# Reordering the ramp of a two-layer pipeline: early grams, products between delta chunks, a packed block stored in halves, weight pieces spread out

## The chip, the cores and the metric

The kernel runs on one core of one Trainium2 chip. The metric is the device time of one launch in microseconds. Three runs of the kernel before gave 913.12, 915.89 and 917.56 us: median 915.89.

## The reference, cut to what matters

Input is x of shape (4, 1024, 128): 4 sequences, 1024 tokens, 128 channels. Two layers follow, each an attention-like block and a feed-forward block, each with a residual and a layer norm behind it.

```python
# layer 0, attention: a delta rule with 4 heads of 32, in chunks of 32 tokens
q, k, v = (silu(causal_depthwise_conv(x @ W.T, taps)) for W, taps in ...)   # 4 taps
beta = sigmoid(x @ Wb.T); q, k = l2norm(q), l2norm(k); v, k_beta = v * beta, k * beta
attn = -(k_beta @ k.T) * strictly_lower                 # per chunk, 32 x 32: the "gram"
for i in range(1, 32): attn[i] += attn[i] @ attn        # the "solve", row by row
u, w = (attn + I) @ v, (attn + I) @ k_beta
for each chunk: u_new = u_i - w_i @ S; o_i = q_i @ S + attn_i @ u_new; S = S + k_i.T @ u_new
# o is mixed with v by a gate, normed by head, and goes through Wo
# layer 0, feed-forward: 8 experts (128 -> 256 -> 128, gelu), the best two weighted by a router
# layer 1, attention: a gated linear scan over time; a = exp(-8 softplus(a_param) sigmoid(..))
# layer 1, feed-forward: a gated unit 128 -> 512, two hidden 512 x 512 layers, 512 -> 128
```

## The kernel before, in words

The tokens are cut into NT = 8 tiles of 128 tokens of all 4 sequences, 512 columns each; channels lie on the partitions. Every fp32 product is made of three matmuls on parts (high times low, low times high, high times high; mm3), so activations and weights are split into a high and a low half by DVE, ACT and POOL.

**Stages.** Five engines each run their own written-out order of instructions (PE, ACT, DVE, POOL, and SP for the DMAs); they meet only in semaphores. The **lead** (for t in range(LEAD), LEAD = 5, in each engine's block) prepares tiles 0 to 4: project (q, k, v products with 12 matmuls each, banks 0 to 2), beta (bank 3), squares (banks 4 and 5), the norms on ACT (norms_ln, norms_exp), unit_rows (q and k scaled, transposed) and value_rows, key_spread (the keys copied per head on ACT, L826), gram (16 matmuls of 128x64 in two halves g = 0, 1, banks 6 and 7, L460), and gram_rows (DVE reads the grams out). The result is a packed block pks[t] that store_pack (L322) writes to memory in one DMA of 1280 KB.

Two tiles together go through a **solve** on POOL (L1090): 31 steps of a multiply and a subtract, each step needing the one before. solve_in (L1269) turns the grams for it, solve_out (L1276) turns its result back and scales it. Solve 0 is for tiles 0 and 1, solve 1 for 2 and 3, solve 2 for 4 and 5, solve 3 for 6 and 7. From its result t_spread (POOL, texp) makes the stationary operands of the delta rule.

**schedule** (L265) then runs, on every engine: ramp1(a=0, s=5), ramp2(a=0, s=6), dense(0, a=1), ramp3(m=0, a=1, s=7), dense(1, ...), tails and so on. a is the tile whose delta rule or attention end is computed, s the tile that is prepared, m the tile in the experts, f the tile in the last feed-forward. ramp1 runs the four chunks of tile 0's delta rule (delta_wu, delta_attn, delta_state on PE; delta_spread, delta_qp, delta_out on DVE; then mix, mix_end) around the preparation of tile 5. ramp2 does the head norm, attention_out, the layer norm, router, top_two, gate_weights and gate_rows of tile 0 around tile 6. dense(m, a, f) loops over the 8 experts: up, gate_rows, one step of tile a's delta rule, down of the expert before; ACT makes two gelus of each half, one in high precision (hf) and one rounded (fbh); DVE subtracts for fbl slot 0, POOL for slot 1. ramp3 is like ramp2, with tile 7 and the scan of layer 1.

**Weights** come in 19 pieces of 512 columns through two buffers (ws); load_piece (SP, L315) waits until DVE has split the piece before in the same buffer (split_pieces, L1297). Pieces 0 to 3 and 8 are centred or scaled as well (five DVE instructions instead of two). PIECES (L33) says which tile's step splits which pieces. load_xs brings a tile of x, split_x splits it.

**Shared memory.** pk2, the packed block of tiles 4 to 7 (12288 bytes a partition), lies over fbh (8192 bytes at at_fb) and the first two slots of fbl behind it; so the first rounded gelu of dense(0) waits for the store of tile 6's block (L977), and that of dense(1) for tile 7's. PE enters dense(0) only when gram_read of tile 6 is complete (L661). softplus_log (L1324) is a chain of 24 DVE instructions on one column; its result, spv, is first used by lru_decay (ACT, L891) in ramp3.

Of the kernel before, what the change touches and what calls it, by code (L numbers as in the profile page):

```python
# [14 lines left out]
NH, DK, C = 4, 32, 32  # L15
# [17 lines left out]
PIECES = ((0, 1), (2, 3), (4, 5), (6, 7, 8), (9, 10, 11), (12,), (13, 14, 15), (16, 17, 18))  # L33
PIECE_BUF = tuple(p % 2 for p in range(NPIECE))
LEAD = 5

# [10 lines left out]
def build(nc, io):  # L47
    ctx = ExitStack()
    with ctx:
# [73 lines left out]
        fbh = sb("fbh", [128, FC, W], F32R); fbl = sb("fbl", [128, FC, W], F32R)  # L123
# [59 lines left out]
        def low_of(p):  # L183
# [3 lines left out]
        names = """w_in cst_in conv_in x_in pk_stored pk_loaded tb_in fw_in ws_in0 ws_in1 ws_hi ws_lo xs_in tt_stored  # L187
            ws_sum ws_mean ws_cen s3_row s3_read cen_ready w3_scaled wo_sum wo_mean wo_cen
            wtap_f wtap_hi wtap_done xt_hi xt_ready
            beta_proj qkv_proj qkv_act sq_done ss_done rs_ln rs_act kq_done kt_done vt_done kexp_done gram_done  # L190
# [60 lines left out]
        def x_slot(t):  # L251
            return 1 if t % 2 == 0 and t < LEAD else 0

# [35 lines left out]
        def _(sp):  # L289
# [32 lines left out]
            def store_pack(t):  # L322
                need(sp, "gram_read", 2 * t + 2)
                need(sp, "kt_done", t + 1)
                need(sp, "vt_done", t + 1)
                need(sp, "pk_stored", 16 * (t - 1))
                sp.dma_start(io["pack"][:, t * CT:(t + 1) * CT, :, :], pks[t][:, :, 1:, :]).then_inc(S["pk_stored"], 16)
# [19 lines left out]
            for t in range(LEAD - 1):  # L347
                load_xs(t + 2)
                for p in PIECES[t][2:] + PIECES[t + 1][:2]:
                    load_piece(p)  # L350
                if t:
                    store_pack(t)
            for p in PIECES[LEAD - 1][2:]:
                load_piece(p)
# [9 lines left out]
            def ramp1(a, s):  # L364
                load_xs(s + 1)
                for p in PIECES[s]:
                    load_piece(p)
                store_pack(s)

            def ramp2(a, s):  # L370
                for p in PIECES[s][:2]:
                    load_piece(p)
                load_xs(s + 1)
                load_next(a + 1)
                store_tt(1)
                for p in PIECES[s][2:] + PIECES[s + 1][:2]:
                    load_piece(p)
# [6 lines left out]
            def dense(m, a, f, inv=0):  # L384
                if isinstance(m, int) and m == 0:
                    load_piece(PIECES[NT - 1][2])
# [19 lines left out]
        def _(pe):  # L406
# [13 lines left out]
            def beta(t):  # L420

                pe.wait_ge(S["xs_in"], 16 * t + 16)
                if t < LEAD:
                    need(pe, "bt_ready", t)
                    bk = 3
                else:
# [3 lines left out]
                    bk = 7  # L430
                mm(by_seq(bank[bk][:, :]), wsm[:, 0, :], xs[:, :, HALO:HALO + TOK]).then_inc(S["beta_proj"], 1)

            def project(t, m):

                pe.wait_ge(S["xt_ready"], t + 1)
                if t < LEAD:
# [5 lines left out]
                else:  # L442
# [3 lines left out]
                o = m if t < LEAD else 4 + m  # L446
# [6 lines left out]
            def squares(t):  # L453

                for m in range(2):
                    pe.wait_ge(S["sq_done"], 2 * t + m + 1)
                    need(pe, "rs_ln", 2 * (t - 1) + m + 1)
# [1288 lines left out]
```

## Time and profile before

| | us |
|---|---|
| median of 3 runs | 915.89 |
| profiled execution | 913.16 |
| its span, first to last instruction | 911.2 |
| PE busy | 815.4 (89%) |
| DVE busy | 618.1 (68%) |
| ACT busy | 490.4 (54%) |
| POOL busy | 481.7 (53%) |
[...]

The stages lie as follows: lead to 99.8 us, ramp1 from there to about 141, ramp2 to about 173, dense(0) to about 229, ramp3 to about 275, then dense(1) and the rest. Busy shares are averages over all stages. [...]

### The profile page before, as it was taken

Reading aid. Unit: us, or ns where it says so; the run is one execution under the profiler, and the core shown is the slowest. Engines: PE = TensorE matmul, PEld = TensorE weight load, DVE = VectorE, ACT = ScalarE, POOL = GpSimd, SP = SyncE. Lnnn points to the kernel's source line nnn. Section 1 sums busy time; section 2 is a strip of 40 time slices with the busy share of each in tenths; the row PEclk is TensorE's granted clock in tenths of the full one; section 3 lists DMA queues with packets and bytes.
Section 4 is the critical chain, followed back from the end, with each engine's and each line's share of the span. In section 5 each row is a group of like instructions: output and inputs, shape, how many; then the busy total and the mean of one; then the engine's idle time right before and its main releaser. Section 6 shows DMA issues by size and latency. Waiting matters only on the chain.

```text
span 911.2 us, 11908 instructions
## 1 busy us (share of the span) xinstructions
PE 815.4 (89%) x3810; PEld 627.9 (69%) x3810; DVE 618.1 (68%) x1166; ACT 490.4 (54%) x768; POOL 481.7 (53%) x508
## 2 busy tenths in 40 slices
PE   5998797688858999899989999999999999999996
PEld 3776584576547767776777678767876886766664
DVE  2777975677357768776876687767767767677352
ACT  3877147042744466357535653574466447667553
POOL 0059696577523744983586345435644454266333
PEclk9998799589959999999999999999999999999999
DMA  3143606300302030003000400120020000000000
GB/s 127 47 115 96 184 2 178 111 12 1 82 0 82 1 82 1 1 0 93 1 1 2 116 0 2 27 66 0 0 69 23 0 0 12 1 0 13 1 12 12
DMA packets 37727, 35.81 MB, mean 39 GB/s; under 512 B 1584, under 2 KB 30512, under 8 KB 37680
## 3 DMA queue, kind: packets, MB, share of 16 engines
q1 hardware_dynamic: 37680, 35.22, 13.8%
q8 instruction: 25, 0.41, 0.2%
q14 instruction: 22, 0.18, 0.1%
HBM read 21.85 MB, written 13.37 MB: 39 GB/s over the span
## 4 chain that ended last, share of the span: by engine, by line
PE 56%; DVE 15%; issue 10%; POOL 10%; ACT 6%; DMA 2%; POOLq 0%; DVEq 0%; ACTq 0%; SPq 0%
PE bank L408 56%; POOL tpm L1105 2%; POOL tmp L1102 2%; POOL fbl L1161 2%; POOL acc L1169 2%; DVE sexp L1401 2%; DVE spread L1385 1%; DVE yg L1411 1%; DVE m L1446 1%; POOL fbl L1192 1%; ACT L1056 1%; DMA pack<-pk 1%; POOL fal L1200 1%; DVE fah L1631 1%; DMA ws<-in_wf 1%
## 5 line engine op out<-in xcount | busy, mean ns | idle before, releaser
L975 ACT ACTIVATE hf<-bank 128x512 f32<-128x512 f32 x64 | 38.3, 598 | 178.5 <-PE bank L408 171.1
L1161 POOL TENSOR_TENSOR fbl<-hf,fbh 128x512 fp32r<-128x512 f32 x64 | 81.9, 1280 | 91.1 <-DVE fbh L1574 91.1
L1102 POOL TENSOR_TENSOR tmp<-apm,tpm 128x31 f32<-128x31 f32 (+15 forms) x124 | 77.5, 625 | 52.8 <-DVE apm L1274 45.6
L1192 POOL TENSOR_TENSOR fbl<-hf,fbh 128x512 fp32r<-128x512 f32 x32 | 41.3, 1290 | 103.2 <-DVE fbh L1631 103.2
L408 PEld LDWEIGHTS bank<-pk,spread 128*128 128x128 f32 x640 | 82.3, 206 | 19.6 <-DVE spread L1385 13.8
L408 PE MATMUL bank<-pk,spread 128*128 128x64 f32 x640 | 85.0, 290 | 8.2 <-DVE spread L1385 7.3
L1572 DVE TENSOR_TENSOR fbl<-hf,fbh 128x512 fp32r<-128x512 f32 x64 | 59.5, 930 | 39.3 <-ACT fbh L979 39.2
L1105 POOL TENSOR_TENSOR tpm<-tpm,tmp 128x31 f32<-128x31 f32 (+15 forms) x124 | 77.9, 628 | 9.7
L1169 POOL TENSOR_TENSOR acc<-acc,yg 128x512 f32<-128x512 f32 x48 | 64.4, 1341 | 32.4 <-DVE yg L1411 32.4
L408 PE MATMUL bank<-fal,wfh 128*128 128x512 f32 x160 | 68.3, 427 | 2.7 <-ACT hf L1005 1.6
L1188 POOL TENSOR_TENSOR fal<-hf,fah 128x512 fp32r<-128x512 f32 x32 | 41.7, 1302 | 51.7 <-DVE fah L1626 51.7
L1411 DVE TENSOR_TENSOR yg<-bank,gb 128x512 f32<-128x512 f32 x64 | 43.9, 685 | 34.5 <-PE bank L408 34.4
L408 PE MATMUL bank<-fbl,wmh 128*128 128x512 f32 x128 | 58.7, 459 | 8.3 <-POOL fbl L1161 4.9
L1005 ACT ACTIVATE hf<-bank,vec 128x512 f32<-128x512 f32 x64 | 42.5, 686 | 42.4 <-PE bank L408 42.1
L1200 POOL TENSOR_TENSOR fal<-hf,fah 128x512 fp32r<-128x512 f32 x32 | 41.4, 1299 | 40.6 <-DVE fah L1631 40.6
L408 PE MATMUL bank<-fah,wfh 128*128 128x512 f32 x160 | 62.6, 391 | 0.0
L408 PE MATMUL bank<-fah,wfl 128*128 128x512 f32 x160 | 62.4, 390 | 0.0
L408 PE MATMUL bank<-fbl,wfh 128*128 128x512 f32 x128 | 55.2, 431 | 7.5 <-POOL fbl L1192 7.5
L408 PE MATMUL bank<-x1l,wmh 128*128 128x512 f32 x128 | 55.5, 433 | 2.8 <-ACT fbh L979 1.6
L408 PE MATMUL bank<-x1h,wmh 128*128 128x512 f32 x128 | 52.0, 406 | 0.0
L408 PE MATMUL bank<-x1h,wml 128*128 128x512 f32 x128 | 51.7, 404 | 0.0
L408 PE MATMUL bank<-fbh,wfh 128*128 128x512 f32 x128 | 51.4, 401 | 0.0
(219 smaller groups left out, 2232.7 us busy)
## 6 DMA issues: line engine op xcount, KB each, us to landing
pack<-pk SPq DMA_DIRECT2D x7, 1280.0 KB, 6.8
pk<-pack SPq DMA_DIRECT2D x7, 1280.0 KB, 7.2
ws<-in_wf SPq DMA_DIRECT2D x11, 256.0 KB, 2.9
xs<-in_xh SPq DMA_DIRECT2D x8, 262.0 KB, 3.6
xt<-in_xh SPq DMA_DIRECT2D x8, 262.0 KB, 3.0
ws<-in_wm SPq DMA_DIRECT2D x8, 256.0 KB, 2.7
tt<-ttp SPq DMA_DIRECT2D x4, 512.0 KB, 2.8
out<-f SPq DMA_DIRECT2D x8, 256.0 KB, 2.5
```

The source lines that it names most:

```text
L408: return P.matmul(out, lhsT, rhs, start=start, stop=stop, skip_group_check=skip)
L975: A.activation(hf[:, 0, :], bank[4][:, :], ACT.Gelu).then_inc(S["gelu_done"], 1)
L1005: A.activation(hf[:, o % 2, :], bank[4 + o][:, :], ACT.Gelu, scale=vec[:, v + o:v + o + 1])\
L1102: G.tensor_tensor(m, a, r, ALU.mult).then_inc(S["t_mul"], 1)
L1105: G.tensor_tensor(o, o, m, ALU.subtract).then_inc(S["t_step"], 1)
L1161: G.tensor_tensor(fbl[:, s, :], hf[:, 1, :], f32(fbh[:, s, :]), ALU.subtract)\
L1169: G.tensor_tensor(acc[:, :], (x1 if e == 1 else acc)[:, :], yg[:, (e - 1) % 2, :], ALU.add)\
L1188: G.tensor_tensor(fal[:, c, :], hf[:, c % 2, :], f32(fah[:, c, :]), ALU.subtract)\
L1192: G.tensor_tensor(fbl[:, o, :], hf[:, o % 2, :], f32(fbh[:, o, :]), ALU.subtract)\
L1200: G.tensor_tensor(fal[:, o, :], hf[:, o % 2, :], f32(fah[:, o, :]), ALU.subtract)\
L1411: tt(yg[:, e % 2, :], bank[6][:, :], gb[:, e % 2, :], ALU.mult).then_inc(S["yg_ready"], 1)
L1572: tt(fbl[:, s, :], hf[:, 0, :], f32(fbh[:, s, :]), ALU.subtract).then_inc(S["lo0"], 1)
```

## The change

It reorders the lead and the ramps and moves three kinds of buffers. The list, by engine:

- **Lead, PE:** tile 0's and tile 1's squares, products and grams stand in a new order; the four grams run right behind project(2, 0). In the last round PE also does beta(5), project(5, 0) and project(5, 1). squares(1) uses banks 6 and 7. Tile 5's beta and products use banks 3, 0, 1 and 3; tile 6's beta is in bank 1, its third product in bank 0.
- **Lead, POOL:** it makes the second half of the keys' copies of tiles 0 and 1 (kexp_pool), two instructions of 128x1024.
- **Lead, DVE:** solve_in(0) comes right behind tile 1's grams; solve_out(0) stands in the last round ahead of piece 8 and tile 4's gram_rows; softplus_log leaves for ramp3; split_x(6) comes at the end.
- **ramp1, ramp2:** below in the diff. From ramp2's DVE order solve_out(1), one piece and split_x(7) go to dense(0), solve_in(2) and two pieces go ahead of head_scale. solve_init(2) and the first ten solve steps leave POOL's ramp2 for dense(0).
- **dense(0):** solve_out(1) at e = 1, split_x(7) at e = 3, pieces at e = 2, 4, 5, 6; two solve steps per expert at e = 1 to 6.
- **Packed block:** fbl and fbh change places in memory, and the rounded halves use slots in the other order (high_slot), so that expert 0's do not lie under the block. Blocks 5 < t are stored in two halves (pk_half, pk_stored).

```diff
-PIECES = ((0, 1), (2, 3), (4, 5), (6, 7, 8), (9, 10, 11), (12,), (13, 14, 15), (16, 17, 18))
+PIECES = ((0, 1), (2, 3), (4, 5), (6, 7), (8,), (9, 10), (11, 12, 13), (14, 15, 16), (17, 18))
-        fbh = sb("fbh", [128, FC, W], F32R); fbl = sb("fbl", [128, FC, W], F32R)
+        fbl = sb("fbl", [128, FC, W], F32R); fbh = sb("fbh", [128, FC, W], F32R)
+        def low_slot(e):
+            return (e % 2) * HC
+        def high_slot(e):
+            return ((e + 1) % 2) * HC
...
             def store_pack(t):
+                if t > LEAD:
+                    need(sp, "gram_read", 2 * t + 1)
+                    need(sp, "pk_half", 16 * (t - LEAD - 1))
+                    c0 = 8
+                    sp.dma_start(io["pack"][:, t * CT:t * CT + c0, :, :], pks[t][:, 0:c0, 1:, :])\
+                        .then_inc(S["pk_half"], 16)
                 need(sp, "gram_read", 2 * t + 2)
...
# PE, lead
-            for t in range(LEAD):
+            squares(0)
+            beta(1)
+            project(1, 0)
+            project(1, 1)
+            squares(1)
+            project(1, 2)
+            beta(2)
+            project(2, 0)
+            gram(0, 0)
+            gram(0, 1)
+            gram(1, 0)
+            gram(1, 1)
+            project(2, 1)
+            project(2, 2)
+            for t in range(2, LEAD):
                 squares(t)
...
+                else:
+                    beta(t + 1)
+                    project(t + 1, 0)
+                    project(t + 1, 1)
                 gram(t, 0)
                 gram(t, 1)
# PE, ramp1 (whole, after)
+                project(s, 2)
+                pe.wait_ge(S["qkv_act"], 3 * LEAD + 2)
                 delta_wu(a, 0)
+                squares(s)
                 delta_attn(a, 0)
                 delta_state(a, 0)
                 delta_wu(a, 1)
+                project(s + 1, 0)
                 delta_attn(a, 1)
                 delta_state(a, 1)
                 delta_wu(a, 2)
+                gram(s, 0)
                 delta_attn(a, 2)
                 delta_state(a, 2)
                 delta_wu(a, 3)
+                gram(s, 1)
                 delta_attn(a, 3)
                 delta_state(a, 3)
+                pe.wait_ge(S["qkv_act"], 3 * LEAD + 3)
+                mix_gate(a)
+                beta(s + 1)
                 project(s + 1, 1)
# PE, ramp2: project(s, 2) ahead of attention_out; dense(0) waits for gram_read behind up(m, 0)
# ACT, lead: tiles 0 and 1 together
+            for m in range(3):
+                heads_in(0, m)
+            beta_in(0)
+            heads_in(1, 0)
+            heads_in(1, 1)
+            beta_in(1)
+            A.preload_act_table_set(LN_EXP)
+            norms_ln(0)
+            norms_ln(1)
+            norms_exp(0)
+            norms_exp(1)
...
+            key_spread(0, 0)
+            key_spread(1, 0)
+            heads_in(1, 2)
# ACT, lru_decay, tile 0
+                    act.wait_ge(S["ws_lo"], NPIECE)
+                    act.wait_ge(S["sp_step"], SP_STEPS)
# DVE, lead
+            beta_rows(0)
+            value_rows(0)
+            split_x(2)
+            split_pieces(PIECES[0][:1])
+            beta_rows(1)
+            unit_rows(0)
+            unit_rows(1)
+            split_pieces(PIECES[0][1:2])
+            gram_rows(0, 0)
+            gram_rows(0, 1)
+            gram_rows(1, 0)
+            gram_rows(1, 1)
+            solve_in(0)
...
+                if t == LEAD - 1:
+                    solve_out(0)
+                split_pieces(PIECES[t])
                 gram_rows(t, 0)
                 gram_rows(t, 1)
-            solve_out(0)
-            softplus_log()
+            split_x(LEAD + 1)
# DVE, ramp1
                 delta_spread(a, 0)
-                split_pieces(PIECES[s])
+                beta_rows(s)
...
                 delta_spread(a, 1)
+                split_pieces(PIECES[s][:1])
+                unit_rows(s)
                 delta_qp(a, 1)
-                split_x(s + 1)
...
                 delta_spread(a, 3)
+                split_pieces(PIECES[s][1:])
...
                 mix_end(a)
+                value_rows(s)
                 gram_rows(s, 1)
# DVE, ramp2 (whole, after)
+                solve_in(2)
+                split_pieces(PIECES[s][:2])
                 head_scale(a)
                 unit_rows(s)
+                beta_rows(s)
                 attention_norm(a)
                 top_two(a)
+                value_rows(s)
+                gram_rows(s, 0)
                 gate_weights(a)
+                gram_rows(s, 1)
                 gate_rows(a)
# DVE, ramp3: behind scale("2")
+                split_pieces(PIECES[NT])
+                softplus_log()
# DVE, dense(0)
+                    if isinstance(m, int) and m == 0 and e == 1:
+                        solve_out(1)
+                    if isinstance(m, int) and m == 0 and e == 3:
+                        split_x(NT - 1)
+                    if isinstance(m, int) and m == 0 and e in (2, 4, 5, 6):
+                        p = (2, 4, 5, 6).index(e)
+                        split_pieces((PIECES[NT - 2][2:] + PIECES[NT - 1])[p:p + 1])
...
+                        if e == 0 and isinstance(m, int) and m in (0, 1):
+                            dve.wait_ge(S["pk_half"], 16 * (m + 1))
# POOL, dense(0) and ramp3
+                    if isinstance(m, int) and m == 0 and e == 1:
+                        solve_init(2)
+                    if isinstance(m, int) and m == 0 and 0 < e < E - 1:
+                        solve(2, range(2 * e - 2, 2 * e))
-                solve(2, range(17, C - 1))
+                solve(2, range(12, C - 1))
```

The SP queue follows the new order: load_xs(6) moves into the lead, the pieces are loaded one tile's step ahead of their splits, store_tt(1) and the last four loads of pieces stand in dense(0).

## Rows read from the trace of the kernel before

**Rows 1.** Stretches: us, busy us of PE, PEld, DVE, ACT, POOL, PEclk, DMA share, GB/s

```profile
22.60:53.00 30.40, 30.35 (x151) 23.52 (x152) 23.59 (x50) 25.17 (x44) 0.00 (x0) 1.00 0.19 53
...
99.80:110.10 10.30, 5.07 (x18) 4.34 (x18) 9.42 (x28) 0.00 (x0) 5.65 (x11) 0.67 0.79 230
...
155.20:167.40 12.20, 8.22 (x40) 8.06 (x40) 10.45 (x13) 2.06 (x3) 9.34 (x16) 0.59 0.30 91
...
176.00:184.00 8.00, 6.63 (x23) 5.80 (x23) 1.07 (x1) 1.15 (x3) 0.00 (x0) 0.50 0.62 166
184.00:229.00 45.00, 39.31 (x203) 32.27 (x203) 37.49 (x65) 16.60 (x33) 34.61 (x31) 0.91 0.03 7
```

**Rows 2.** PE's waits, 79 to 330 us: total, times, longest

```profile
PE bank L408 <- DVE gate L1494: 6.1, 1, 6.1
PE bank L408 <- POOL texp L1131: 5.2, 1, 5.2
```

**Rows 3.** POOL timeline, first and last step of solve 0, then texp

```profile
55.05 0.24 POOL L1102 TENSOR_TENSOR tmp<-apm,tpm 128x31 f32<-128x31 f32 x1 [45.56 <-DVE apm L1274]
...
98.21 0.25 POOL L1105 TENSOR_TENSOR tpm<-tpm,tmp 128x31 f32<-128x31 f32 x1
103.79 2.46 POOL L1131 TENSOR_TENSOR texp<-ttp,cst 128x512 f32<-128x512 f32 x2 [5.33 <-DVE ttp L1285]
```

**Rows 4.** DVE timeline, solve 0's input, piece 8, solve 0's output, first spread

```profile
53.00 1.97 DVE L1274 STREAM_TRANSPOSE apm<-kkp 128x1024 f32<-128x1024 f32 x1
...
86.87 1.10 DVE L1304 TENSOR_TENSOR ws<-ws,s3row 128x512 f32<-128x512 f32 x1
...
90.47 0.96 DVE L1312 TENSOR_TENSOR wfl<-ws,wfh 128x512 fp32r<-128x512 f32 x1
...
100.49 1.90 DVE L1283 STREAM_TRANSPOSE ttp<-tpm 128x1024 f32<-128x1024 f32 x1
...
110.12 1.22 DVE L1385 TENSOR_TENSOR spread<-bank,cst 128x1024 f32<-128x1024 f32 x1
```

**Rows 5.** PE timeline, the lead: start, us, engine line op, idle before and releaser

```profile
24.93 0.80 PE L408 MATMUL bank<-xtl,wtaph 128*128 128x512 f32 x1
...
33.58 0.40 PE L408 MATMUL bank<-xth,wtaph 128*128 128x512 f32 x1
33.81 1.89 PE L408 MATMUL bank<-pk,gb 128*128 128x64 f32 x16
```

**Rows 6.** PE timeline, tile 4 and the start of dense(0)

```profile
81.31 1.94 PE L408 MATMUL bank<-hf,cst 128*128 128x512 f32 x4
87.13 3.65 PE L408 MATMUL bank<-pk,gb 128*128 128x64 f32 x16 [3.88 <-DVE pk L1236]
...
184.19 0.76 PE L408 MATMUL bank<-x1l,wmh 128*128 128x512 f32 x1 [1.41 <-ACT fbh L979]
```

**Rows 7.** DVE timeline, end of ramp1 and x1 in ramp2

```profile
138.03 1.01 DVE L1423 SCALAR_TENSOR_TENSOR a<-a,pk 128x512 f32<-128x512 f32 x1
...
153.37 0.69 DVE L1379 TENSOR_TENSOR x<-bank,a 128x512 f32<-128x512 f32 x1 [3.58 <-ACT a L860]
```

**Rows 8.** DVE timeline, router read, gate done, and lru_input in ramp3

```profile
167.37 0.18 DVE L1463 COPY lg<-bank 128x32 f32<-128x32 f32 x1
...
170.98 0.19 DVE L1494 TENSOR_TENSOR gate<-gt 128x32 f32<-128x32 f32 x1
...
241.85 0.90 DVE L1434 SCALAR_TENSOR_TENSOR m<-m,x 128x512 f32<-128x512 f32 x1 [6.33 <-ACT m L887]
```

**Rows 9.** ACT timeline, the first high half of dense(0)

```profile
183.45 0.60 ACT L979 ACTIVATE fbh<-bank 128x512 fp32r<-128x512 f32 x1 [5.05 <-DMA pack<-pk]
```

**Rows 10.** DVE by line and shape, 184 to 229 us: busy, mean ns, idle

```profile
L1411 DVE TENSOR_TENSOR yg<-bank,gb 128x512 f32<-128x512 f32 x8 | 5.5, 685 | 2.2 <-PE bank L408 2.1
...
L1312 DVE TENSOR_TENSOR wfl<-ws,wfh 128x512 fp32r<-128x512 f32 x3 | 4.3, 1421 | 0.1
```

**Rows 11.** POOL timeline, after ramp3

```profile
280.62 1.28 POOL L1161 TENSOR_TENSOR fbl<-hf,fbh 128x512 fp32r<-128x512 f32 x1 [22.31 <-DVE fbh L1574]
```

More of the change, by code:

```diff
@@ L348, in _ @@
                 load_xs(t + 2)
-                for p in PIECES[t][2:] + PIECES[t + 1][:2]:
+                for p in PIECES[t + 1]:
                     load_piece(p)
@@ L352, in _ @@
                     store_pack(t)
-            for p in PIECES[LEAD - 1][2:]:
-                load_piece(p)
+            load_piece(PIECES[LEAD][0])
+            load_xs(LEAD + 1)
             store_pack(LEAD - 1)
@@ L364, in ramp1 @@
             def ramp1(a, s):
-                load_xs(s + 1)
-                for p in PIECES[s]:
+                load_piece(PIECES[s][1])
+                for p in PIECES[s + 1][:2]:
                     load_piece(p)
@@ L385, in dense @@
                 if isinstance(m, int) and m == 0:
-                    load_piece(PIECES[NT - 1][2])
+                    store_tt(1)
+                    for p in PIECES[NT - 1][1:] + PIECES[NT]:
+                        load_piece(p)
                 if inv == 1:
@@ L605, in ramp1 @@
                 delta_wu(a, 2)
-                squares(s)
+                gram(s, 0)
                 delta_attn(a, 2)
@@ L809, in beta_in @@
                     act.wait_ge(*after("d2", 1))
-                A.activation(btanh[slot(t)], bank[3 if t < LEAD else 7][:, :], ACT.Tanh, scale=0.5).then_inc(S["bt_ready"], 1)
+                A.activation(btanh[slot(t)], bank[beta_bank(t)][:, :], ACT.Tanh, scale=0.5).then_inc(S["bt_ready"], 1)
             def norms_ln(t):
@@ L836, in _ @@
             act.wait_ge(S["w_in"], 32)
-            for t in range(LEAD):
+            for m in range(3):
[9 more added lines that the diff above has]
+            norms_exp(1)
+            act.wait_ge(S["sp_step"], 1)
+            A.activation(spv[:, 1:2], spv[:, 0:1], ACT.Exp, scale=-1.0).then_inc(S["sp_step"], 1)
+            key_spread(0, 0)
+            key_spread(1, 0)
+            heads_in(1, 2)
+            for t in range(2, LEAD):
                 for m in range(3):
@@ L908, in ramp1 @@
             def ramp1(a, s):
-                for c in range(3):
-                    heads_in(s, c)
                 beta_in(s)
+                heads_in(s, 0)
+                heads_in(s, 1)
                 A.preload_act_table_set(LN_EXP)
@@ L1119, in _ @@
             solve_init(0)
+            for t in range(2):
+                pool.wait_ge(S["kq_done"], 2 * t + 2)
+                G.tensor_tensor(kspread[slot(t)][1], rep(pks[t][:, 8:16, SK:SK + 1, :], 2, NH), heads(8), ALU.mult)\
+                    .then_inc(S["kexp_pool"], 1)
             solve(0, range(C - 1))
@@ L1144, in ramp2 @@
             def ramp2(a, s):
-                solve_init(2)
                 t_spread(a + 1, 0)
                 t_spread(a + 1, 1)
-                solve(2, range(10))
             def ramp3(m, a, s):
@@ L1174, in dense @@
                         solve_init(3)
-                    if isinstance(m, int) and m == 0 and e < E - 1:
-                        solve(2, range(10 + e, 11 + e))
+                    if isinstance(m, int) and m == 0 and e == 1:
+                        solve_init(2)
+                    if isinstance(m, int) and m == 0 and 0 < e < E - 1:
+                        solve(2, range(2 * e - 2, 2 * e))
                     if inv == 1 and e >= 3:
@@ L1353, in _ @@
             centre_rows(wsm[:, 2:3, :], wsum[:, 20:21], "wo", 1)
-            for t in range(LEAD):
+            beta_rows(0)
[11 more added lines that the diff above has]
+            solve_in(0)
+            value_rows(1)
+            split_x(3)
+            split_pieces(PIECES[1][:2])
+            for t in range(2, LEAD):
                 unit_rows(t)
                 if t == LEAD - 1:
-                    split_pieces(PIECES[t - 1][2:])
                     solve_in(1)
```

129 lines of the change are left out of this document (61 added, 68 removed).

## The prediction

> **What bounds the kernel now.** I read three views in this order. The table by stretches shows that the lead is TensorE's own: 30.35 of 30.40 us busy at full clock [rows 1]. The ramp after it is not: between 99.8 and 110.1 PE works 5.07 of 10.3 us, between 155.2 and 167.4 it waits much of the time while DVE is busy for 10.45 of 12.2 us, and from 176 to 184 everything except PE stands nearly still and PE runs at half clock (PEclk 0.50) [rows 1]. PE's waits name what it waited for longest: the gate from DVE and texp from POOL [rows 2]. The timelines then say why those two came late. From about 276 us on, PE is close to full and the change alters nothing in what is computed, so what the ramp saves or loses is simply carried to the end; my sum is over the stretch to 276 us, plus one short term behind it. It is made against the profiled execution (913.16 us, span 911.2) and moved to the median of the runs, 915.89, which is 2.7 higher.
>
> **A. The lead.** POOL's solve 0 runs from 55.05 to 98.46, 43.4 us [rows 3], and starts when DVE has turned the grams of tiles 0 and 1 (53.00 plus 1.97) [rows 4]. In the new order PE does squares(0), beta(1), two products of tile 1, squares(1), its third product, beta(2), one product of tile 2, then the four grams. One product is a third of 24.93 to 33.81, 2.9 us; one gram 1.8 [rows 5]. PE starts on squares(0) at 22.6; the two first products of tile 1 end near 30.6, and squares(1) waits 0.4 us for ACT. With squares(1) and two more products PE is ready for gram(0,0) at 39.0. For tile 4 the way from squares to the first gram is 5.8 us [rows 6]; from squares(1) near 32, with two tiles' logarithms, exponentials and key copies behind each other on ACT (about 2.5 us more), it ends at 40.4. PE idles 1.4 us there. Four grams at 1.8, the second pair held by 0.3 us because DVE splits piece 1 ahead of their reading, end at 47.6; reading and turning (0.8 and 1.97) give 50.35, so solve 0 starts at 50.4, 4.6 us sooner, and ends at 93.9. The second halves of the key copies go to POOL, which is idle there until 55.05 [rows 3]. The bounds of this start are 2 us sooner and not sooner at all. PE's price is 1.3 us later at squares(4), which nothing waits for: tile 4's grams are read only at 101.7 (below).
>
> DVE now waits for solve 0 with solve_out(0) ahead of piece 8: turning and scaling take 3.2 us (from 100.49 until POOL is released at 103.7 [rows 3, 4]) and end at 97.1. Then come piece 8 (86.87 to 91.4, 4.6 us), two gram reads (1.5), split_x(6) (1.2), and delta_spread(0) starts at 104.3. The small chain of softplus (from 103.6 to 110.1 [rows 4]) is gone from here. Before it was 110.12: **A = -5.8**, ends -3 and -8.
>
> **B. ramp1.** From the first spread to the end of mix_end are 28.9 us [rows 4, 7]. PE meanwhile has done tile 5's third product and squares(5), so it idles from 102 to 105.5, and after an idle of 3.88 us a gram took 3.65 instead of 1.89 us [rows 5, 6]: 16 small matmuls of the first chunk at half clock cost 1.7 us more. On DVE a second piece comes into the chain and split_x and value_rows go out of it: 0.9 more. **B = +2.6**, ends 0 and +5. The chain on DVE goes on being the bound; less PE work lies between the chunks, but that was not what they waited for.
>
> **C. mix_end to x1** (139.0 to 153.4, [rows 7]). Behind the last chunk PE had gram(5,1) and two products (7.6 us) ahead of head_sums; now mix_gate, beta(6) and one product (4.3): 3.3 sooner, and the head's exponential goes ahead of tile 6's logarithms, 1.2 sooner. But DVE now has value_rows, a gram read, solve_in(2) and two pieces (0.7, 0.8, 2.0 and 2.8, 6.3 us) between mix_end and head_scale, where it was idle: by my count head_scale waits 2.7 us for them. **C = -1.8**, ends -4.5 and +2.
>
> **D. x1 to the gate** (153.37 to 171.17, [rows 7, 8]). From 155.2 to 167.4 DVE did solve_out(1), solve_in(2), three pieces with a wait for one's transfer, and split_x(7) before it read the router's product [rows 1, 8]: 12.2 us go. In come value_rows and one gram read ahead of gate_weights (1.5), and the router's own time, hidden before (0.6). **D = -10.1**, ends -7 and -12.
>
> **E. Gate to up(0,1)** (171.2 to 184.19, [rows 6, 8]). ACT waited 5.05 us for the packed block's store until 183.45 [rows 9], and PE's last gap 1.41 us for that gelu [rows 6]. Now the first high half goes to a slot that the block does not cover, and the first low half needs the first half of the store. That is issued at the first gram read, 2 us ahead of the rest; I put the half at 5 us (whole: 7.4), landing 3 us before it is asked for. What is late next is PE itself: the 10.4 us it was busy here were at half clock. If the denser ramp keeps full clock they take 5.4 (saving 6.6 with the gap), if not, only the gap of 1.4 goes. I take **E = -4.5**, between the two, nearer to full clock because the long gap before gate_turn (6.1 [rows 2]) shrinks to about 1. up(0,1) then starts 19.6 us sooner.
>
> **F. dense(0).** This is where the moved work goes. DVE was busy 37.49 of 45 us [rows 1]. Out go three pieces (1.42 and 0.54 each, 5.9 [rows 10]); in come four (7.9), solve_out(1) (3.1) and split_x(7) (1.5): 44.1 of 45. POOL was busy 34.61 [rows 1]; seven long solve steps (13.1) are replaced by twelve short ones and a clearing (17 to 20): 39 to 42. Two engines without slack in a chain that hands every expert from ACT to DVE and POOL to PE do not stay at 45: **F = +3.5**, ends 0 (all of it fits in DVE's idle) and +9 (all 6.6, stretched).
>
> What speaks against F here: DVE's subtract with both operands in SBUF takes 1421 ns beside a busy POOL, while the one that reads PSUM stays at 685 [rows 10]. [...]
>
> **G, H. ramp3 and dense(1).** Softplus and two pieces now stand in ramp3 ahead of lru_input, 6.9 to 9.7 us of DVE work where DVE was idle for 6.33 us before 241.85 [rows 8]; lru_decay on ACT waits for them and the norm of the attention is queued behind it, but it began 2.6 us after that point: G = 0 to +1, I take 0.3. Nineteen solve steps instead of fourteen on POOL are some 8 us more, ahead of an instruction before which POOL was idle for 22.31 us [rows 11]. In dense(1) the same split store saves some 0.8 of ACT's wait: H = -0.8. The SP queue issues one piece transfer after another behind waits on DVE's splits; each is loaded one piece ahead, so I count it at nothing; a miss costs one landing, about 3 us.
>
> **Sum**: -5.8 + 2.6 - 1.8 - 10.1 - 4.5 + 3.5 + 0.3 - 0.8 = -16.6. Profiled 896.6; median 915.89 - 16.6 = **899.3**.
>
> **Rivals.** (1) dense(0) takes back most: DVE and POOL bound it, F = +9, and E saves only its gap (-1.4): 915.9 - 8 = 908, up to 912. For it: DVE 44 of 45 us. Chance 0.12. (2) The early grams do not start the solve sooner (ACT's double chain or DVE's piece holds gram(0,0) by 5 us): A loses 4.6, 904. It is the case in which the title's first item does nothing. Chance 0.07. (3) More: the ramp keeps full clock and DVE's idle takes the moved work: E = -6.6, F = 0, B = 0: 891. Chance 0.08. [...] Chance 0.05.
>
> **Numbers.** My forecast has 0.68, between 893 and 907. The range that leaves 2 in 10 out is 888 to 911. Below 0.5% (4.6 us, about what can be told from no change) lies a part of rival 1: faster 0.88, same 0.07, slower 0.05.
>
> **What would show it.** Solve 0's first step near 50.4 (A wrong if after 53); first spread near 104; mix_end's end near 136; gate near 156; no wait of ACT for the pack store; dense(0), from up(0,1) to head_sums, 48 to 49 us with DVE over 42 busy; lru_decay not held by softplus for more than 1 us. The prediction is wrong if PEclk stays at 0.5 from the first to the last stage of the ramp, or if dense(0) exceeds 55 us.

## The result, and the profile after

The changed kernel takes 910.17 us, the median of 20 runs (903.21 to 915.05), against 915.82 for 20 runs of the kernel before on the same chip: a ratio of 0.9939, 95% interval 0.9921 to 0.9956. That is 5.6 us faster where I had forecast 16.6. The sign held, the size did not: 910.17 lies outside the 893 to 907 to which I gave 0.68, and only just inside the wide range, 888 to 911. The profiled execution after took 905.48 us (span 903.5, clock 0.944), 7.7 less than the 913.16 profiled before (clock 0.946).

The table by stretches for the kernel after (us, then busy us of PE, PEld, DVE, ACT, POOL, then PEclk, which is TensorE's mean granted clock with 1.00 for full speed, DMA share, GB/s), to be held against [rows 1]:

```profile
23.90:48.60 24.70, 20.78 (x93) 14.85 (x93) 17.64 (x31) 15.65 (x29) 4.73 (x2) 0.98 0.08 22
48.60:57.00 8.40, 8.40 (x36) 8.11 (x37) 2.54 (x7) 0.00 (x0) 0.00 (x0) 0.50 0.22 63
...
113.20:143.50 30.30, 28.24 (x180) 25.36 (x180) 22.61 (x48) 8.02 (x16) 27.48 (x41) 0.89 0.31 87
...
156.20:163.30 7.10, 5.13 (x31) 4.75 (x30) 6.74 (x30) 4.91 (x8) 2.49 (x2) 0.77 0.51 168
...
163.30:171.90 8.60, 8.51 (x39) 6.95 (x40) 5.08 (x11) 2.17 (x4) 0.90 (x1) 0.59 0.57 152
171.90:220.20 48.30, 39.41 (x205) 32.30 (x204) 42.57 (x67) 16.02 (x31) 37.38 (x43) 0.93 0.11 34
220.20:267.30 47.10, 34.84 (x117) 23.25 (x118) 30.42 (x78) 28.61 (x43) 25.25 (x40) 0.70 0.24 63
```

The first two lines are the lead from squares(0) to the last gram's reading, the third is ramp1 (B), and the last four are x1 to gate (D), gate to up(0,1) (E), dense(0) (F) and ramp3 (G). Those of D, E and F are close to what these terms said. The first two are not: the lead, at full clock throughout before (PEclk 1.00 [rows 1]), now has 8.4 us at PEclk 0.50. The same marks in both profiled executions. The row of A gives the time of the first spread, the others the length of the stage:

| stage | before | after | difference | forecast |
|---|---|---|---|---|
| A: first spread | 110.12 | 113.25 | +3.1 | -5.8 |
| B: to mix_end's end | 28.9 | 30.3 | +1.4 | +2.6 |
| C: to x1 | 14.3 | 12.7 | -1.6 | -1.8 |
| D: to the gate | 17.8 | 7.1 | -10.7 | -10.1 |
| E: to up(0,1) | 13.0 | 8.6 | -4.4 | -4.5 |
| F: dense(0) | 45.1 | 48.3 | +3.2 | +3.5 |
| G: ramp3, to the next spread | 45.8 | 47.1 | +1.3 | +0.3 |
| sum, to 267.3 | 275.1 | 267.3 | -7.8 | -15.8 |

8.0 us are missing in the sum, and the first line alone is 8.9 off; the others together are 0.9 better than forecast. From there to the end of the span it is 636.2 us after and 636.1 before. The timelines show how it went. First VectorE, from the norms of tile 1 to solve_in(0) (start, us, engine, line, operation, in brackets the idle time before and who ended it):

```profile
39.10 0.68 DVE L1312 TENSOR_TENSOR pk<-q,hf 128x512 f32<-128x512 f32 x1
39.70 0.70 DVE L1314 STREAM_TRANSPOSE pk<-pk 128x512 f32<-128x512 f32 x1
40.33 3.06 DVE L1312 TENSOR_TENSOR pk<-a,a 128x512 f32<-128x512 f32 x2
43.31 0.70 DVE L1314 STREAM_TRANSPOSE pk<-pk 128x512 f32<-128x512 f32 x1
43.94 0.64 DVE L1367 TENSOR_REDUCE wsum<-ws 128x4 f32<-128x512 f32 x1
44.61 1.23 DVE L1369 TENSOR_SCALAR wsum<-wsum 128x4 f32<-128x4 f32 x1
...
47.67 0.42 DVE L1339 TENSOR_TENSOR pk<-bank,cst 128x256 f32<-128x256 f32 x1
48.01 0.41 DVE L1341 TENSOR_TENSOR kkp<-bank,beta_tok 128x256 f32<-128x256 f32 x1
...
52.25 0.42 DVE L1339 TENSOR_TENSOR pk<-bank,cst 128x256 f32<-128x256 f32 x1 [3.17 <-PE bank L433]
...
56.45 2.01 DVE L1350 STREAM_TRANSPOSE apm<-kkp 128x1024 f32<-128x1024 f32 x1
```

Then POOL, which makes the second halves of the two key copies:

```profile
39.86 2.38 POOL L1194 TENSOR_TENSOR spread<-pk,cst 128x1024 f32<-128x1024 f32 x1 [30.40 <-DVE pk L1312]
43.47 2.35 POOL L1194 TENSOR_TENSOR texp<-pk,cst 128x1024 f32<-128x1024 f32 x1 [1.23 <-DVE pk L1312]
58.54 0.24 POOL L1174 TENSOR_TENSOR tmp<-apm,tpm 128x31 f32<-128x31 f32 x1 [12.72 <-DVE apm L1350]
```

And TensorE, the four early grams in order:

```profile
41.79 1.97 PE L433 MATMUL bank<-pk,gb 128*128 128x64 f32 x16 [0.39 <-issue]
43.60 1.95 PE L433 MATMUL bank<-pk,spread 128*128 128x64 f32 x16
48.57 3.64 PE L433 MATMUL bank<-pk,spread 128*128 128x64 f32 x16 [3.02 <-DVE kkp L1341]
52.01 3.62 PE L433 MATMUL bank<-pk,texp 128*128 128x64 f32 x16
```

What to see: while POOL's first copy runs (39.86 to 42.24), VectorE's two multiplications with both operands in SBUF take 3.06 us in place of 1.25 (E2); while the second runs (43.47 to 45.82), a scalar operation on four columns takes 1.23 us in place of 0.17 (E2) and ends with it (45.84). Behind these, weight piece 1 (43.94 to 47.75) stands ahead of the reading of tile 0's grams, and TensorE's third gram waits for that reading, 3.02 us. Then it runs at half clock (PEclk 0.50 from 48.6 to 57.0 us): 3.64 and 3.62 us for the last two grams in place of 1.96. VectorE waits for them in its turn (3.17 and 2.66 us). Solve 0 starts at 58.54 where I had 50.4 and where it was 55.05 before [rows 3]. Part of this belongs to the execution and not to the change. TensorE's first products in the lead were slow for longer, with 0.63 us for one matmul up to 16.3 us and 0.40 behind it where before it was 0.63 up to 14.0, so squares(0) began at 23.92 us where it was 22.65 before; in E8 and E11, whose lead is the same as after, it began at 22.96 and 22.62. Counted from squares(0), the first spread came after 87.5 us before and 89.3 after.

Two more lengths vary between profiled executions and not by a change in them. Ramp1 takes 30.3 us after and 31.5 in E8 and E11. From ramp3's end to the end of the span it is 635.7 to 636.8 us (before, after, E2, E3, E4, E7) or 638.7 to 639.3 (E1, E5, E6, E8 to E11). So one pair of profiled executions shows no stage difference below some 1.3 us, and no total below 3.

### The profile page after: what moved, and what is told of

The parts are those of the page before. It is cut to its first block, busy times and chain, and to the rows that moved or that the text cites. A ratio compares the mean times of both kernels' runs of the same rounds, so it can differ in the third digit from the quotient of the medians.

```text
span 903.5 us, 11902 instructions
## 1 busy us (share of the span) xinstructions
PE 820.6 (91%) x3810; PEld 633.3 (70%) x3810; DVE 625.1 (69%) x1166; ACT 484.3 (54%) x758; POOL 487.1 (54%) x510
## 4 chain that ended last, share of the span: by engine, by line
PE 53%; DVE 23%; ACT 8%; issue 7%; POOL 6%; DMA 2%; DVEq 0%; SPq 0%; POOLq 0%; ACTq 0%
PE bank L433 53%; DVE sexp L1489 2%; DVE spread L1473 2%; DMA xs<-in_xh 2%; DVE m L1534 1%; DVE yg L1499 1%; POOL fbl L1235 1%; POOL acc L1243 1%; POOL tpm L1177 1%; POOL fbl L1268 1%; DVE pk L1312 1%; POOL tmp L1174 1%; DVE ttp L1359 1%; ACT L1128 1%; DVE fbh L1669 1%
## 5 line engine op out<-in xcount | busy, mean ns | idle before, releaser
L1174 POOL TENSOR_TENSOR tmp<-apm,tpm 128x31 f32<-128x31 f32 (+15 forms) x124 | 77.8, 627 | 20.2 <-DVE apm L1350 12.7
L1077 ACT ACTIVATE hf<-bank,vec 128x512 f32<-128x512 f32 x64 | 42.5, 687 | 45.1 <-PE bank L433 44.9
L1276 POOL TENSOR_TENSOR fal<-hf,fah 128x512 fp32r<-128x512 f32 x32 | 41.3, 1293 | 43.5 <-DVE fah L1726 43.5
L433 PE MATMUL bank<-fbh,wfl 128*128 128x512 f32 x128 | 52.5, 410 | 0.0
```

The source lines that it names most:

```text
L433: return P.matmul(out, lhsT, rhs, start=start, stop=stop, skip_group_check=skip)
L1077: A.activation(hf[:, o % 2, :], bank[4 + o][:, :], ACT.Gelu, scale=vec[:, v + o:v + o + 1])\
L1174: G.tensor_tensor(m, a, r, ALU.mult).then_inc(S["t_mul"], 1)
L1276: G.tensor_tensor(fal[:, o, :], hf[:, o % 2, :], f32(fah[:, o, :]), ALU.subtract)\
```

## The experiments

All were timed in five rounds beside the kernel before. E1 to E4 change the kernel after in one thing, E5 joins the mends (E1, E2 and E4), E6 and E7 leave one part of that out, E8 and E11 take a part of the change away from the kernel after, E9 and E10 start from E5. Where runs of different rounds are compared, the ratio to the kernel before in the same rounds is what counts.

**E1, pieces 0 and 1 earlier.** VectorE splits both ahead of its wait for the s3 row, where it has nothing to do.

```
+            split_pieces(PIECES[0])
             dve.wait_ge(S["s3_row"], 1)
 ...
-            split_pieces(PIECES[0][:1])
 ...
-            split_pieces(PIECES[0][1:2])
```

> The changed kernel, with DVE splitting pieces 0 and 1 in its idle stretch before 23.6 us instead of piece 0 ahead of beta_rows(1) and piece 1 ahead of the first gram read. Theory (the lead failed: the copies of the keys on POOL and piece 1 on DVE hold the grams of tile 1, PE idles 3.0 us and falls to half clock): PE's gap before gram(1,0) shrinks under 1 us, the four grams take 1.9 us each, POOL's first solve step comes at about 51 to 53 instead of 58.5, the first spread at about 107 instead of 113.3, and the time falls by 5 to 7 us, to about 904 (ratio to before 0.987). Rival (the solve is not what holds the ramp; DVE's queue and the late x transfers hold it): the first solve step moves but the first spread stays within 2 us of 113.3, time 908 to 911.

**E2, all key copies on ACT**, as before; POOL does nothing in the lead.

```
             key_spread(0, 0)
+            key_spread(0, 1)
             key_spread(1, 0)
+            key_spread(1, 1)
 ...
-            for t in range(2):      # POOL
-                pool.wait_ge(S["kq_done"], 2 * t + 2)
-                G.tensor_tensor(kspread[slot(t)][1], ...
```

> The changed kernel, with the second halves of the copied keys of tiles 0 and 1 made by ACT (8 activations, 3.4 us) as before, not by POOL. Theory of contention: unit_rows(1)'s two multiplies take 1.4 us again instead of 3.06, and the small scalar instruction that took 1.23 us takes 0.17; the gram read of tile 0 comes 2.8 us sooner (44.9), PE's gap before gram(1,0) is below 1 us and the clock does not fall; first solve step at about 53 to 54, time about 905. Rival (POOL's copies were not what held it; ACT's longer chain now holds the grams): PE's gap moves to gram(0,1) or gram(1,1) and the time is 910 or more.

Measured: E1 907.32 us (901.54 to 908.39), ratio 0.9886 [0.9855, 0.9916]; E2 904.01, 0.9864 [0.9831, 0.9896]. VectorE's timeline for E1 and then for E2:

```profile
39.76 3.07 DVE L1312 TENSOR_TENSOR pk<-a,a 128x512 f32<-128x512 f32 x2
...
49.38 2.07 DVE L1350 STREAM_TRANSPOSE apm<-kkp 128x1024 f32<-128x1024 f32 x1
```

```profile
39.31 1.25 DVE L1307 TENSOR_TENSOR pk<-a,a 128x512 f32<-128x512 f32 x2
41.11 0.65 DVE L1362 TENSOR_REDUCE wsum<-ws 128x4 f32<-128x512 f32 x1
41.79 0.17 DVE L1364 TENSOR_SCALAR wsum<-wsum 128x4 f32<-128x4 f32 x1
...
49.27 2.08 DVE L1345 STREAM_TRANSPOSE apm<-kkp 128x1024 f32<-128x1024 f32 x1
```

VectorE's timelines show both mends. Without POOL's copies the same two multiplications take 1.25 us and the four-column operation 0.17; with them and with the piece out of the way they are as slow as ever (3.07), but nothing hangs on them. Either mend alone brings solve_in(0) from 56.45 to 49.3, the grams back to 1.97 us, and the first spread to 105.68 (E1) and 105.32 (E2), close to the 104.3 of my sum. Counted from squares(0), which began 0.6 and 1.0 us sooner here, they give back 7.0 and 6.9 us of the 7.6 to 7.9. So the miss needs both: the copy holds VectorE, and the piece stands between that and the gram's reading. Yet the medians fell by only 2.9 and 6.2 us, by the ratios 4.9 and 6.9; for E1 I had expected 5 to 7. Most of the rest was given back in ramp3 (first E1, then E2):

```profile
216.90:266.70 49.80, 34.89 (x117) 22.80 (x118) 31.80 (x78) 28.54 (x43) 25.60 (x40) 0.71 0.23 59
```

```profile
214.60:264.70 50.10, 36.44 (x117) 24.21 (x118) 31.81 (x79) 28.58 (x43) 25.63 (x40) 0.67 0.23 59
```

Both lost 1.2 to 1.3 us in ramp1, the variation named above, and E1 lost 1.4 more between gate and up(0,1) (10.0 us, all at PEclk 0.50) and 1.7 in dense(0).

**E3, the lead's old order** (grams of tiles 0 and 1 where they were, the old places of the pieces, all copies on ACT), all else as after.

```
-            squares(0) ... gram(0, 0) gram(0, 1) gram(1, 0) gram(1, 1) ...
-            for t in range(2, LEAD):
+            for t in range(LEAD):
                 squares(t)
```

> The changed kernel with the order of the kernel before for tiles 0 and 1 in the lead (no early grams, key copies on ACT), everything behind it as changed. Theory: the early grams cost instead of helping, by PE's 3.0 us gap and 8 us of half clock; without them the first solve step is at about 55, squares(4) at about 81 to 82, the first spread at 108 to 110, and the time is 2 to 5 us below the changed kernel's 910, about 906. Rival (the early grams gave what the change gained; the rest of the change gave nothing): time at or above 915.

Measured: 905.37 us (899.01 to 915.71), 0.9894 [0.9866, 0.9923]. Solve_in at 52.75, first spread at 106.62. The lead stays at full clock (30.6 us at PEclk 1.00). Against the old order the lead of the change costs 6.6 us at the first spread (5.1 counted from squares(0)), and 4.8 in the median, 4.1 by the ratios; the two ratio intervals just touch.

**E4, softplus early**, at 13 to 18 us, where VectorE waits for TensorE's s3 row; it leaves ramp3. ACT makes the exponential for it ahead of the first product.

```
+            softplus_log()
             dve.wait_ge(S["s3_row"], 1)
 ...
-                softplus_log()
                 lru_input(m)
```

> The changed kernel, with the exponential and the chain of softplus done in DVE's idle stretch ahead of 23.6 us instead of in ramp3. Theory: in ramp3 this chain took 8.1 us ahead of lru_input and made ramp3 1.6 us longer; without it ramp3 is 2 to 3 us shorter and the time about 907.5 to 908.5. If the chain is too long for the idle stretch, squares(0) starts up to 2 us later and the gain is gone. Rival (ramp3 is bound by ACT and PE, DVE's work there is hidden): no change, 910.

Measured: 905.78 us, 0.989 [0.9867, 0.9914]. The reason for it is in the timeline of the kernel after, VectorE in ramp3, where every instruction of the chain works on a single column:

```profile
228.39 0.16 DVE L1409 TENSOR_TENSOR spv<-spv 128x1 f32<-128x1 f32 x1
228.58 0.15 DVE L1410 TENSOR_SCALAR spv<-spv 128x1 f32<-128x1 f32 x1
228.77 1.01 DVE L1409 TENSOR_TENSOR spv<-spv 128x1 f32<-128x1 f32 x1
...
234.02 0.48 DVE L1411 TENSOR_TENSOR spv<-spv 128x1 f32<-128x1 f32 x1
234.53 0.15 DVE L1412 TENSOR_SCALAR spv<-vec 128x1 f32<-128x1 f32 x1
```

and in POOL's at the same time:

```profile
228.49 2.50 POOL L1207 TENSOR_TENSOR texp<-tb,cst 128x512 f32<-128x512 f32 x2 [11.52 <-DMA tb<-tt]
230.94 0.63 POOL L1174 TENSOR_TENSOR tmp<-apm,tpm 128x247 f32<-128x247 f32 x1
```

Here the instruction with two operands in SBUF takes 0.16 us while POOL is idle and 0.36 to 1.01 beside it; the one with one operand stays at 0.15 (228.58, 229.82 us). In E4, where POOL has no work at that time, every one with two operands takes 0.16. The chain takes 8.1 us (227.4 to 235.5), in E4 4.4. But ramp3 itself, 47.1 us after, is 47.0 in E4: the chain's length was not what bounded it in this execution. E4's gain of 4.4 us in the median is larger than what its stages show for softplus, and larger than the 2 to 3 that I had expected. The first spread came at 110.56 in place of 113.25; of these 2.7 us, 1.2 are squares(0)'s start (22.71 against 23.92) and 0.8 a third gram that was at half clock for only a part (2.86 us; PEclk 1.00 to 48 us, 0.61 from there to 49, 0.50 behind it).

**E5, E6, E7: the mends together.** E5 joins E1, E2 and softplus (behind split_x(2), its exponential as in E4); E6 has them with the lead's old order, E7 with the copies left on POOL.

```
+            split_pieces(PIECES[0])
             dve.wait_ge(S["s3_row"], 1)
 ...
             split_x(2)
+            softplus_log()
             beta_rows(1)
```

> The changed kernel with three of the single edits together: key copies on ACT, pieces 0 and 1 in DVE's idle stretch before 22 us, softplus behind split_x(2) with its exponential ahead of the first product. Theory: two terms of the sum had failed, the lead (A, -5.8 forecast, +3.1 seen) and softplus in ramp3 (G, +0.3 forecast, +1.6 seen, 4 in the two runs whose lead was mended). With both mended the first spread is at about 104 to 106, ramp3 is at most 46 us, and the time is about 899 to 902, what the forecast gave. Rival (a repaired lead is given back at half clock later): first spread at 105 but the time stays at 904 or more, with ramp3 or dense(0) longer.

> As the last, but with the order of the kernel before for tiles 0 and 1 in the lead (no early grams). Theory: the solve starts at 55 and ends at about 96.5, which is 1.5 to 2 us after the early version's 95; DVE's queue ahead of solve_out(0) hides none of it, so the first spread is 1 to 2 us later and the time about 900 to 903, 1 to 2 above the early version. Rival (an unbroken PE in the lead is worth more than an earlier solve): equal to it or faster, with the higher mean clock.

> As the first of these, but the key copies stay on POOL. Theory: with no piece between, POOL's hold of unit_rows(1) (3.06 instead of 1.4 us) costs under 1 us in the start of the solve; the time is within 1.5 us of the version with ACT, about 900 to 903. Rival (ACT's 3.4 us more are what matters): faster than the version with ACT by 2 us or more.

| run | median us | ratio to before | solve_in | first spread | gate | up(0,1) | ramp3 |
|---|---|---|---|---|---|---|---|
| after | 910.17 | 0.9939 [0.9921, 0.9956] | 56.45 | 113.25 | 163.34 | 171.90 | 47.1 |
| E5 | 898.52 | 0.9818 [0.9796, 0.9839] | 49.68 | 105.72 | 155.52 | 164.43 | 47.1 |
| E6 | 903.88 | 0.9861 [0.9834, 0.9889] | 54.08 | 107.94 | 157.81 | 166.75 | 47.1 |
| E7 | 900.41 | 0.9846 [0.9822, 0.9869] | 48.96 | 104.96 | 156.31 | 166.30 | 46.4 |

E5 (897.42 to 902.07) beats both kernels and stands 0.8 us from the forecast of 899.3. That is in part luck: its stages to the end of ramp3 sum to 14.0 us saved where I had 15.8, softplus is not where the forecast had it, and its profiled execution took 902.07 where I had 896.6. E6 against E5 says what early grams are worth once nothing holds them: 2.2 us at the first spread, with squares(0) at the same time (23.73 and 23.75), and 4 us by the ratios (0.9861 against 0.9818, the intervals overlap a little), where I had expected 1 to 2. E7 against E5: the copies on POOL bring nothing; by the ratios they cost 2.6 us, with overlapping intervals, so only "no gain" is shown. E7 against E1 differs in softplus and its exponential alone: 46.4 us of ramp3 in place of 49.8. TensorE's timelines of ramp3 show a wait ahead of the router, E1 first, then E2:

```profile
238.64 1.06 PE L433 MATMUL bank<-wr,x 128*128 128x8 f32 x8 [2.76 <-DVE x L1466]
```

```profile
236.54 1.88 PE L433 MATMUL bank<-wr,x 128*128 128x8 f32 x8 [2.31 <-DVE x L1462]
```

Router waits of over 2 us stand in E1, E2 and E8, whose ramp3 takes 49.8 to 50.1 us; in the kernel after, E3 and E11, with the same softplus and 46.9 to 47.4 us, they are 0.18, 0.84 and 1.88. What it waits for goes back to ACT's first instruction of lru_decay, which reads softplus's result. The kernel after, then E1, and VectorE's last split ahead of softplus in E1:

```profile
235.71 0.82 ACT L961 ACTIVATE m<-m,spv 128x512 f32<-128x512 f32 x1 [0.41 <-issue]
```

```profile
235.04 0.81 ACT L961 ACTIVATE m<-m,spv 128x512 f32<-128x512 f32 x1 [2.99 <-issue]
```

```profile
224.54 1.67 DVE L1388 TENSOR_TENSOR wfl<-ws,wfh 128x512 fp32r<-128x512 f32 x1
```

ACT's instruction starts 0.09 us after the chain has ended in both. ACT was ready 15.1 us after head_sums after and 15.2 in E1; the chain ended 15.4 and 18.1 us after it. The 2.7 us between are 1.1 of a later start of VectorE's work behind head_sums, which took TensorE 1.90 us at PEclk 0.56 in place of 1.13 at 1.00, 1.0 of this split (0.69 us after), which ran beside texp on POOL (224.28 to 227.33), and 0.6 of the chain. The wait is 1.07 us in E3, 2.11 in E11, 2.54 in E2 and 3.13 in E8. So softplus in ramp3 costs nothing or some 3 us, as the clock and POOL's steps fall.

**E8 and E11, the packed block's store.** E8 stores it whole again; E11 does that and puts the gelu's halves back in the slots of before, with ACT's old wait.

```
-                if t > LEAD:        # first half of the block ahead of the rest
 ...
-            return ((e + 1) % 2) * HC      # E11
+            return (e % 2) * HC
```

> The changed kernel with the packed block of tiles 6 and 7 stored whole, as before, and DVE's first low half waiting for the whole store; the order of the slots stays changed. Theory: the store starts at about 164 and lands at 171.5; the first low half (169.7) and all behind it in dense(0) wait 1.5 to 2 us: up(0,1) is unmoved, dense(0) about 1.5 us longer, time 911 to 912. Rival (the half store is what released dense(0)): up(0,1) 3 us or more later, time 914.

> The changed kernel with the packed block's part undone: one whole store, fbh ahead of fbl and the slots in the old order, ACT's first rounded gelu of dense(0) waiting for the store. Theory: the store, issued near 164, lands at 171.5, 3 us after ACT could have made this gelu; but PE is busy at half clock until 171.9 anyway, so up(0,1) starts only about 1 us later, time 910 to 912. Rival (the wait for the store was worth the whole 4.5 us of term E): up(0,1) at 175 or later, time 914 or more.

Measured: E8 910.09 us (908.61 to 913.66), 0.9951 [0.9933, 0.9969]; E11 910.24 (907.84 to 915.24), 0.9949 [0.9925, 0.9973]. Neither can be told from the kernel after. ACT's timeline of E11 at the first high half, to be held against [rows 9], and TensorE's stretches from gate to up(0,1), E11's and then those of the kernel before:

```profile
168.11 0.60 ACT L1045 ACTIVATE hf<-bank 128x512 f32<-128x512 f32 x1 [7.91 <-PE bank L433]
170.04 0.60 ACT L1049 ACTIVATE fbh<-bank 128x512 fp32r<-128x512 f32 x1 [1.34 <-DMA pack<-pk]
```

```profile
162.80:172.10 9.30, 9.19 (x40) 7.63 (x40) 4.74 (x11) 2.17 (x4) 0.32 (x1) 0.55 0.53 141
```

```profile
171.20:184.20 13.00, 10.42 (x40) 8.54 (x40) 5.80 (x11) 1.35 (x3) 1.62 (x3) 0.50 0.38 102
```

Even with the old slots and one store, ACT waits 1.34 us in place of 5.05, and TensorE, busy 9.19 of 9.30 us, does not wait for it. The store can be issued once VectorE has read the block's last gram. In E11 that reading ends 0.7 us after the gate (163.52 against 162.85), in the kernel before it ended 4.8 us after it (175.93 against 171.17).

**E9, the moved work back in ramp2**, on top of E5: solve_out(1), pieces and split_x(7) ahead of the router's reading again.

```
                 attention_norm(a)
+                solve_out(1)
+                split_pieces(PIECES[s][2:])
+                split_x(s + 1)
                 top_two(a)
```

> The mended version (898.5, key copies on ACT, pieces 0 and 1 and softplus early), with the work that the change moved out of DVE's ramp2 put back ahead of top_two: solve_out(1), one piece, split_x(7); in dense(0) DVE keeps three pieces. Theory (D was right, and dense(0) gives back about 3 us of it): the gate comes 6 to 8 us later, dense(0) is 2 to 4 us shorter, time 903 to 905. Rival (the moved work costs in dense(0) what it saved in ramp2): time within 2 us of 898.5.

Measured: 901.34 us, 0.9837 [0.9812, 0.9861]. The stretches x1 to gate and dense(0), of E5 and then of E9:

```profile
148.30:155.50 7.20, 5.84 (x31) 5.45 (x30) 6.51 (x29) 4.90 (x8) 2.48 (x2) 0.59 0.51 169
...
164.40:214.00 49.60, 41.27 (x205) 33.39 (x204) 42.23 (x67) 15.93 (x31) 36.99 (x43) 0.90 0.11 33
```

```profile
149.00:161.10 12.10, 5.48 (x31) 5.09 (x30) 11.63 (x36) 4.92 (x8) 2.48 (x2) 0.58 0.33 107
...
169.60:214.70 45.10, 36.90 (x207) 30.13 (x205) 37.98 (x61) 16.19 (x31) 37.81 (x43) 0.94 0.06 19
```

The gate comes 4.9 us later after x1 (I had expected 6 to 8), and dense(0) is 4.5 us shorter (2 to 4 expected); head_sums starts at 214.68 against 214.03. That part of D is an exchange with dense(0): 4.9 us against 4.5, nothing by the profiled executions and 1.7 by the two ratios, whose intervals overlap. The rest of D (12.1 us in E9 against 17.8 before) is solve_in(2) and the first pieces, which E9 leaves where VectorE was idle ahead of head_scale; that part was not undone by itself; by these stages it should be the one that pays, which is argued and not shown.

**E10, piece 16 from dense(0) to ramp3**, on top of E5.

```
-(11, 12, 13), (14, 15, 16), (17, 18))
+(11, 12, 13), (14, 15), (16, 17, 18))
```

> The mended version, with piece 16 split in ramp3 instead of dense(0), e = 6. Theory (DVE is the bound of dense(0), busy about 43.5 of 50 us, and idle for 6 us in ramp3): dense(0) gets 1 to 2 us shorter and ramp3 no longer, time 897 to 898. Rival (POOL or PE's clock bounds dense(0), or the piece's transfer is late in ramp3): no change or up to 3 us longer.

Measured: 901.03 us, 0.984 [0.9817, 0.9863]: dense(0) 48.5 us (49.6 in E5), ramp3 48.0 (47.1). I had expected 897 to 898 and ramp3 no longer. What it frees in one it costs in the other; no gain.

## Why the prediction came out too low

**A failed, and with it the size.** The step reads "the second pair held by 0.3 us because DVE splits piece 1 ahead of their reading", with the copies on "POOL, which is idle there". Measured: TensorE was held by 3.02 us, and the last two grams ran at half clock. From my 50.4 to 58.54: squares(0) began 1.3 us later than in the execution I had; the wait was 2.7 longer; the two grams took 3.5 more (7.06 in place of 3.6); the rest, 0.6, lies in small steps. The end of the solve kept its distance (43.5 us), and the first spread came at 113.25 in place of 104.3: 9 us, of which E1 and E2 give back 7.6 to 7.9 (7.0 and 6.9 counted from squares(0)). What I had asked of POOL was whether it had time, not what its instruction does to VectorE beside it. I had noted a slow subtract beside a busy POOL in dense(0) (1421 ns [rows 10]) and weighed it for dense(0) alone. The trace of before had the price in it, at the end of solve 0, where a one-column multiplication of the softplus chain ran beside texp on POOL [rows 3]:

```profile
103.75 0.16 DVE L1328 RECIPROCAL spv<-spv 128x1 f32<-128x1 f32 x1
103.95 1.10 DVE L1329 TENSOR_TENSOR spv<-spv 128x1 f32<-128x1 f32 x1
105.09 1.18 DVE L1330 TENSOR_TENSOR spv<-spv 128x1 f32<-128x1 f32 x1
```

The two TENSOR_TENSOR end at 105.05 and 106.27 us, the two texp instructions at 105.02 and 106.25 (the first taken as half of their 2.46 us). The lead after shows the same with more columns: beside POOL's copies 3.06 us for two multiplications in place of 1.25, and 1.23 in place of 0.17 for a `tensor_scalar` of four columns; a `tensor_scalar` of a single column stayed at 0.15 beside texp (228.58 us after).

Rival 2 was this case ("ACT's double chain or DVE's piece holds gram(0,0) by 5 us", 904, 0.07). Its effect, a solve that does not start sooner, came true; its place was the third gram, and it was worse than its price, since the solve started later than before.

**B** was +1.4 for +2.6, and +2.6 in E8 and E11 with the same code, so this execution does not tell the two apart; some half clock was there (PEclk 0.89 over the stage). **C** and **D** held within 0.6 us, **F** within 0.3, with VectorE busy for 42.57 us where I had asked for over 42, and POOL for 37.38 where I had 39 to 42. E9 bears out that VectorE's load moves dense(0): 4.2 us less of it made the stage 4.5 shorter. E9 corrects how D and F belong together: 4.9 us of D are F seen from the other end.

**E** gave its number largely by luck. Of the 4.4 us, 2.5 are idle time of TensorE that is gone (10.42 busy of 13.00, against 8.51 of 8.60) and 1.9 a later part at full clock (PEclk 1.00 from 170.5 us). But neither the halves nor the slots took the idle time away: E8 and E11, without them, stay at 910.1 and 910.2. What is left as its cause is the earlier reading of the grams, part of D's move; that is argued, since it was not undone alone. The clock's share varies: gate to up(0,1) took 8.6 us after, 9.1 in E2, and 10.0 in E1, E7 and E8, these three at PEclk 0.50 throughout.

**G** was +1.3 for +0.3, but not by softplus: E4, E5 and E6, without it, have ramp3 at 47.0 and 47.1 us too, and what the 1.3 is stays open. I took softplus as 6.9 to 9.7 us with the pieces; together they took 10.3 and softplus alone 8.1, by the same holding. My sign, lru_decay held for at most 1 us, came true in the profiled execution (0.41), but not in the other five kernels with softplus in ramp3 (1.07 to 3.13). E7 against E1 puts it at 3 us in one pair, and E4 against the kernel after at nothing in another.

**H** gave nothing for -0.8: 636.2 us behind ramp3 for 636.1.

**From 7.8 to 5.6.** The profiled execution after was among its faster ones: the 20 runs span 12 us and mostly go with the clock (905.48 and 905.88 at 0.944, 914.29 and 915.05 at 0.935 and 0.933), those of the kernel before 6.5. How much of that spread comes from the lead's half-clock stretch is not settled; E5, without it, spans 4.7 us, E3, also without it, 16.7.

**Rivals 1 and 3.** Dense(0) took back 3.2, not 9; PE was not at full clock through the ramp (PEclk 0.89, 0.77 and 0.59 in B, D and E). The last 0.05 was for a kernel slower than before; it is 5.6 us faster, and dense(0), at 48.3 us, stays under the 55 that would have made the prediction wrong.

What stays open: why E4 gained 4.4 us in the median when its stages show less. The profiled execution of the kernel after may be one of few with a short wait of lru_decay, as the 2.11 to 3.13 us in E8 and E11 suggest; its other runs have no profile.

## What to carry to other kernels

Before giving work to an idle GpSimd, look up what VectorE does beside it. Here VectorE instructions with two operands in SBUF, even of one column (1.10 and 1.18 us in place of 0.16), ended with the texp instruction on GpSimd beside them or after it; in the lead after two such multiplications took 3.06 us in place of 1.25, and with a weight piece behind them TensorE lost both the wait (3.02 us) and its clock (8.4 us at PEclk 0.50). Filler such as a weight piece goes where nobody waits for the engine, never directly ahead of a reading that releases TensorE. Work moved out of a waiting stage into a full one was paid again there (E9: 4.9 us against 4.5), work moved into an idle stretch was not (E1's pieces): count the two destinations apart.

## What the runs showed of the hardware that I had not expected

A gap of 3.02 us in TensorE's work was followed by 8.4 us at PEclk 0.50; in E1 and E2, with gaps of at most 0.38 us ahead of the grams, the grams stayed at 1.95 to 1.97 us. The half-clock time was about as dear as the wait itself: 3.5 us for the two grams behind a wait of 3.0. A late input was hidden in a stretch that was mostly at half clock: in E11 ACT's store wait of 1.34 us left TensorE idle for only 0.11 of 9.30 us, at PEclk 0.55. And the held VectorE instructions ended with GpSimd's or after it, small ones too: the one-column multiplication at 228.77 us ended at 229.78, the first of the two texp instructions at 229.74 (half of their 2.50 us); the two multiplications of 512 columns ended at 43.39, 1.15 us behind the copy's end at 42.24, which is about their own time (1.25).
